# SyncE's issue order changed, and the raw feed-forward weights loaded from GpSimd's queue

## The chip, the core and the metric

The kernel runs on one core of a Trainium2 chip. The core has five engines with a queue each: TensorE (PE in the profile) multiplies matrices, VectorE (DVE), ScalarE (ACT) and GpSimd (POOL) work on rows of 128 partitions, and SyncE (SP) computes nothing and issues DMAs. An engine works its queue off in order; where an instruction waits for a semaphore, everything behind it on that engine waits too. The metric is the device time of one execution in microseconds (us), lower is better.

## The reference

x is [4, 512, 512]. It is normalised and attends, with 32 heads of 16 columns and an axial rotation of q and k, over a context [4, 512, 256]; then comes a feed-forward block whose two weight matrices are cut to three values.

```
q = rope((layernorm(x) @ Wq)); k, v = split(ctx @ Wkv); k = rope(k)
w = softmax(q k^T / 4);  x = x + (w v) @ Wout + bout
xn = layer_norm(layernorm(x));  x_hat = absmax_quant(xn)           # 8 bits
w_hat = sign(round(w / (mean|w| + 1e-6))) * mean|w|                # ternary
h = gelu(x_hat @ w_fc_hat^T);  x = x + absmax_quant(layer_norm(h)) @ w_proj_hat^T
```

All in float32 from outside; the kernel splits float32 operands into bf16 or float32r parts to multiply them exactly enough.

## The kernel before

There are three stages.

Projection (0 to about 150 us): 16 tiles of 128 rows. q and k are rotated, turned, split in three bf16 parts and stored to DRAM (`store_parts`, L270, twelve DMAs for every second tile) from buffers that lie in `ternary_words`, the memory that later holds the turned ternary weights.

Attention (about 140 to 500 us): 32 groups of 4 heads, a batch being 8 groups. For each pair of groups the parts come back as stacks (`load_stacks`, L658): a lower half in 7 DMAs, an upper half in 8, of which the first 3 are q and the last 5 are k. They go round three slots. On TensorE step s does group s - 2. For a group it computes

- scores (`scores`, L748) only to find each row's maximum, one group or more ahead; VectorE reduces them (`row_maxima`, L871);
- scores turned (`scores_turned`, L779), with the row maximum subtracted by two extra rows of the stack; ScalarE takes exponentials;
- the product with the values (`weigh_v`, L795), four chunks in a group, of which the first two are done in the second half of the group's own step and the last two in the first half of the next step.

The maxima take a long way round. GpSimd negates and splits them (`split_maxima`, L902 to L908), SyncE turns them by a DMA transpose (`turn_max`, L668) and stores them into the stack (`load_max`, L672); `scores_turned` of the group waits for that. GpSimd also copies the values of each group into place (`stage_v`, L930), for which `weigh_v` waits.

Beside this a 32nd of the feed-forward weights is made ternary in each step: the raw weights are loaded (`load_weight`, L679 even numbers, w_fc; L682 odd ones, w_proj; two slots), GpSimd cuts them (`ternarise`, L917, L919, L922, two slots of output), SyncE turns them into `ternary_words` by a DMA transpose (`turn_weight`, L688). The second operation of `ternarise(n)` waits until `turn_weight(n - 2)` has landed, and `load_weight(n)` waits for `ternarise(n - 2)`. Since `ternary_words` held the parts, SyncE waits for all stores of parts before the first `turn_weight`.

Finally the rows stage (about 485 us to the end), output product, feed-forward, residuals, in which TensorE is busy nearly throughout.

All orders are written out by hand, one queue for each engine at the end of the kernel. Of SyncE's queue the part from s == TILES + 4 of the first loop and the second loop matter, of GpSimd's the part from `set_pads(pool, 1)`. In a step SyncE issues turn_max, half a pair of stacks, load_max, the raw weight, the sums' transfers (`pack_sums`) and turn_weight. GpSimd does stage_v, split_maxima, ternarise and, in every second step from step 10, a division (L935).

## Time and profile before

| | us |
|---|---|
| median of 3 runs (760.91 to 762.63) | 761.99 |
| the profiled execution's own time | 762.23 |
| its span, first to last instruction | 760.4 |
| TensorE busy in the span | 734.2 |
| VectorE, ScalarE, GpSimd busy | 656.8, 457.1, 432.6 |

The profiled execution spends 1.8 us outside its span. PE is TensorE's matmuls, PEld its weight loads, which overlap them. In the views "SPq" is SyncE issuing a DMA, whose time is that of the issue and not of the transfer. A releaser, written "<-", is what ended an engine's wait. The clock column is TensorE's granted share of full speed: 1.00 is 2.4 GHz, 0.50 is 1.2 GHz.

### The profile page before, as it was taken

How to read it: one execution, taken by the hardware profiler on the slowest of the kernel's cores; microseconds unless marked ns; L12 is line 12 of the kernel's file. 1: busy time of each engine (PE TensorE's matmuls, PEld its weight loads, DVE VectorE, ACT ScalarE, POOL GpSimd, SP SyncE). 2: the span in 40 equal slices, each digit the busy share in tenths (PEclk: the TensorE clock that was granted, in tenths of full speed). 3: DMA queues.
4: the chain of work that ended last, by engine and by line, in shares of the span. 5: the costliest groups of instructions: out<-in, count | busy, mean ns of one | idle time of the engine just before them, and what ended most of it. 6: DMA issues, size and time to landing. Idle time of an engine off the chain costs nothing.

```text
span 760.4 us, 11891 instructions
## 1 busy us (share of the span) xinstructions
PE 734.2 (97%) x3886; PEld 313.9 (41%) x3886; DVE 656.8 (86%) x927; ACT 457.1 (60%) x830; POOL 432.6 (57%) x502
## 2 busy tenths in 40 slices
PE   5999999979999999999999999999999999999998
PEld 3787777412222222222222122445555555555443
DVE  6787998878999999989989787379999889998895
ACT  4786766756777777777777688764224432333330
POOL 5787776754555556654555486466474745663310
PEclk9999999989999999999999999999999999999999
DMA  8798998666577778889888785426657665545546
GB/s 278 191 239 231 256 246 195 150 146 181 137 163 169 166 162 167 162 157 182 151 168 172 171 160 117 94 57 137 119 118 125 119 145 117 105 97 105 117 97 139
DMA packets 185715, 118.05 MB, mean 155 GB/s; under 512 B 120068, under 2 KB 150836, under 8 KB 185652
## 3 DMA queue, kind: packets, MB, share of 16 engines
q1 hardware_dynamic: 185654, 117.29, 69.1%
q8 instruction: 31, 0.51, 0.3%
q14 instruction: 30, 0.25, 0.1%
HBM read 64.50 MB, written 25.43 MB: 118 GB/s over the span
## 4 chain that ended last, share of the span: by engine, by line
PE 77%; SPq 7%; DMA 6%; DVE 3%; issue 2%; ACT 2%; POOL 2%; POOLq 0%; DVEq 0%; ACTq 0%
PE banks L1116 15%; PE banks L1101 15%; PE banks L779 12%; PE banks L795 11%; PE banks L310 9%; PE banks L748 6%; PE banks L1082 6%; SPq L658 4%; DMA stack_words<-k_parts 3%; DVE maxima L871 2%; SPq L270 1%; PE banks L341 1%; DMA late_words<-k_parts 1%; SPq L668 1%; PE banks L765 1%
## 5 line engine op out<-in xcount | busy, mean ns | idle before, releaser
L891 ACT ACTIVATE probs_words<-banks 128x512 f32<-128x512 f32 x512 | 266.0, 603 | 85.9 <-PE banks L779 85.7
L871 DVE TENSOR_REDUCE maxima<-banks 128x2 f32<-128x1024 f32 x240 | 278.4, 1214 | 32.6 <-PE banks L748 31.5
L795 PE MATMUL banks<-probs_words,late_words 128*32 128x512 f32 x1024 | 137.8, 611 | 0.4 <-ACT probs_words L891 0.2
L1101 PE MATMUL banks<-ternary_words,late_words 128*128 128x512 f16 x512 | 113.1, 379 | 0.0
L1116 PE MATMUL banks<-ternary_words,stack_words 128*128 128x512 f16 x512 | 112.9, 379 | 0.0
L779 PE MATMUL banks<-stack_words 114*128 114x512 bf16 x352 | 105.1, 390 | 4.1 <-DMA stack_words<-max_rows 3.9
L1300 ACT ACTIVATE probs_words<-probs_words,h_moments 128x2048 f32<-128x2048 f32 (+1 forms) x17 | 32.2, 1902 | 121.3 <-DVE h_moments L1179 121.3
L1101 PEld LDWEIGHTS banks<-ternary_words,late_words 128*128 128x128 f16 x512 | 49.9, 98 | 60.5 <-issue 0.8
L1116 PEld LDWEIGHTS banks<-ternary_words,stack_words 128*128 128x128 f16 x512 | 49.2, 98 | 60.7 <-issue 2.9
L779 PEld LDWEIGHTS banks<-stack_words 114*128 114x128 bf16 x352 | 26.8, 97 | 91.2 <-ACT probs_words L891 71.4
L1294 ACT ACTIVATE probs_words<-banks,row_scale 128x512 f32<-128x512 f32 x64 | 43.0, 685 | 30.7 <-PE banks L1101 30.7
L748 PE MATMUL banks<-stack_words 48*128 48x512 bf16 x320 | 55.8, 384 | 3.9 <-DMA stack_words<-k_parts 2.1
L902 POOL TENSOR_SCALAR neg_max<-maxima 128x16 f32<-128x16 f32 x32 | 8.3, 260 | 85.1 <-DVE maxima L871 85.1
L1307 POOL TENSOR_TENSOR v_words<-v_words 128x512 f32<-128x512 f32 x16 | 27.0, 1687 | 50.0 <-DMA v_words<-in_x_dram 50.0
L917 POOL TENSOR_SCALAR late_words<-late_words,limits 128x512 f16<-128x512 f32 x32 | 50.2, 1568 | 7.3 <-DMA late_words<-in_L_ffn_w_fc_dram 7.3
L1322 POOL TENSOR_SCALAR v_words<-v_words 128x512 f32<-128x512 f32 x14 | 36.9, 2637 | 26.0 <-DVE late_words L1161 26.0
L544 POOL TENSOR_TENSOR ternary_words<-attn_words,ternary_words 128x512 bf16<-128x512 f32 x32 | 37.3, 1167 | 23.3 <-ACT ternary_words L497 22.6
L919 POOL TENSOR_SCALAR late_words<-late_words,limits 128x512 f16<-128x512 f32 x32 | 50.3, 1572 | 0.0
L779 PE MATMUL banks<-late_words 114*128 114x512 bf16 x160 | 47.0, 384 | 0.0
L540 POOL TENSOR_TENSOR attn_words<-attn_words 128x512 f32<-128x512 f32 x32 | 41.4, 1293 | 2.1 <-DVE attn_words L422 1.9
L748 PEld LDWEIGHTS banks<-stack_words 48*128 48x128 bf16 x320 | 12.7, 93 | 69.6 <-DVE maxima L871 53.4
L1174 DVE BATCH_NORM_STATS2 h_stats<-probs_words 128x6 f32<-128x512 f32 x64 | 39.4, 678 | 0.0
(162 smaller groups left out, 1129.9 us busy)
## 6 DMA issues: line engine op xcount, KB each, us to landing
o_rows<-late_words SPq DMA_DIRECT2D x32, 256.0 KB, 2.9
k_parts<-ternary_words SPq DMA_DIRECT2D x48, 128.0 KB, 3.4
q_parts<-ternary_words SPq DMA_DIRECT2D x48, 128.0 KB, 2.6
stack_words<-q_parts SPq DMA_DIRECT2D x22, 192.0 KB, 3.1
attn_words<-in_x_dram SPq DMA_DIRECT2D x16, 256.0 KB, 5.0
probs_words<-in_L_ffn_w_fc_dram SPq DMA_DIRECT2D x16, 256.0 KB, 3.5
probs_words<-in_L_ffn_w_proj_dram SPq DMA_DIRECT2D x16, 256.0 KB, 5.3
late_words<-in_L_ffn_w_fc_dram SPq DMA_DIRECT2D x16, 256.0 KB, 3.7
```

Of the source, the lines that this page charges most:

```text
L310: mm = self.nc.tensor.matmul(out, lhs[a][:, slot, k * P:(k + 1) * P], rhs[b][:, k, :], start=(a + b + k == 0), stop=(a == 1 and k == count ...
L748: mm = self.nc.tensor.matmul(self.score_slot[j % 2][:, half], self.stack(0, g)[rows, head, c * P:(c + 1) * P], self.stack(1, g)[rows, head ...
L779: self.nc.tensor.matmul(self.st_bank[(g * 16 + k) % self.ST_BANKS], self.stack(1, g)[0:STACK, head, c * P:(c + 1) * P], self.stack(0, g)[0 ...
L795: mm = self.nc.tensor.matmul(self.pv_bank[32 * j:32 * j + 32], self.v_ones[:, g % 2, c, j, :], self.probs[:, c, j, :], start=(c == 0), sto ...
L871: dve.tensor_reduce(self.maxima[:, g % 2].rearrange("p (x i) -> p x i", x=2)[:, :, j], self.score_slot[j % 2], AX.X, ALU.max).then_inc(sel ...
L891: act.activation(self.probs[:, c, head, :], self.st_bank[(g * 16 + k) % self.ST_BANKS], ACT.Exp, scale=1 / math.sqrt(HEAD)).then_inc(self. ...
L917: pool.tensor_scalar(self.below[:], self.raw[:, w], limits[:, 1, w:w + 1], None, ALU.is_lt).then_inc(self.cut, 1)
L919: pool.tensor_scalar(self.ternary[:, w], self.raw[:, w], limits[:, 0, w:w + 1], None, ALU.is_gt).then_inc(self.cut, 1)
L1082: mm = self.nc.tensor.matmul(self.y_bank[n % 2], self.mixT[n % 2][a][:, k], self.wout_parts[b][:, k, :], start=(a + b + k == 0), stop=(a = ...
L1101: mm = self.nc.tensor.matmul(self.fc_bank[o], self.uT[:, n % U_SLOTS, part * KX + k], self.fcT[:, k, o], start=(k + part == 0), stop=(k == ...
L1116: mm = self.nc.tensor.matmul(self.proj_bank[r], self.hT[:, r, part, k], self.projT[:, k // 2, k % 2], start=(k + part == 0), stop=(part == ...
L1294: act.activation(self.h[:, n % H_SLOTS, o * DIM:(o + 1) * DIM], self.fc_bank[o], ACT.Gelu, scale=self.row_scale[:, n % U_SLOTS]).then_inc( ...
```

## The change

Four things in SyncE's queue, and one that leaves it for GpSimd's.

- Maxima of group 2: turn_max(2) and load_max(2) stood behind the last tile's twelve stores and behind the wait for all stores. Now turn_max(2) stands before these stores and load_max(2) in their middle.
- Upper halves of stacks: all 8 DMAs stood in the even step. Now the 3 of q are issued in the odd step before, behind load_max, and the 5 of k stay.
- Raw weights: the two before the loop and one in each step are gone from SyncE. GpSimd issues them: numbers 0 and 1 behind set_pads(1), and number n + 2 behind ternarise(n).
- The four pieces of Wout are loaded two in each of two steps instead of one in each of four.

TensorE's, VectorE's and ScalarE's queues are the same.

```diff
@@ -259,12 +259,12 @@
-    def store_parts(self, sp, n):
+    def store_parts(self, sp, n, which=slice(0, 2 * PARTS)):
...
-        for s, part in ((0, 0), (0, 1), (1, 0), (0, 2), (1, 1), (1, 2)):
+        for s, part in ((0, 0), (0, 1), (1, 0), (0, 2), (1, 1), (1, 2))[which]:
...
-    def load_stacks(self, sp, pair, half):
+    def load_stacks(self, sp, pair, half, both=(0, 1)):
...
-        for t, where, runs in ((0, mem.q_parts, self.Q_RUNS[half]), (1, mem.k_parts, self.K_RUNS[half])):
+        for t in both:
+            where, runs = ((mem.q_parts, self.Q_RUNS[half]), (mem.k_parts, self.K_RUNS[half]))[t]
...
-    def load_weight(self, sp, w_fc, w_proj, n):
+    def load_weight(self, queue, w_fc, w_proj, n):
         half = n % 4 // 2
-        need(sp, self.ternary_ready, n - 1)
+        need(queue, self.ternary_ready, n - 1)
...
@@ -1373,14 +1374,16 @@
                 if s == TILES + 4:
                     sp.wait_ge(prj.projected[1], TILES)
-                    att.load_weight(sp, w_fc, w_proj, 0)
-                    att.load_weight(sp, w_fc, w_proj, 1)
                     att.turn_max(sp, 1)
                     att.begin_late_stacks(sp)
                     att.load_stacks(sp, STACK_PAIRS - 1, 0)
                     att.load_max(sp, 1)
                     att.load_stacks(sp, STACK_PAIRS - 1, 1)
-                if within(s - 5, TILES) and (s - 5) % 2 == 1:
+                    att.turn_max(sp, 2)
+                    prj.store_parts(sp, TILES - 1, slice(0, PARTS))
+                    att.load_max(sp, 2)
+                    prj.store_parts(sp, TILES - 1, slice(PARTS, 2 * PARTS))
+                if within(s - 5, TILES - 1) and (s - 5) % 2 == 1:
                     prj.store_parts(sp, s - 5)
...
@@ -1394,24 +1397,24 @@
-                if s == 3:
-                    att.turn_max(sp, 2)
-                    att.load_max(sp, 2)
                 if 5 <= s < GROUPS + 2:
                     att.turn_max(sp, s - 2)
-                if 2 * STACK_PAIRS <= s + 1 < GROUPS:
-                    att.load_stacks(sp, (s + 1) // 2, (s + 1) % 2)
+                if 2 * STACK_PAIRS <= s + 1 < GROUPS and s % 2 == 1:
+                    att.load_stacks(sp, (s + 1) // 2, 0)
+                if 2 * STACK_PAIRS <= s < GROUPS and s % 2 == 0:
+                    att.load_stacks(sp, s // 2, 1, (1,))
                 if 5 <= s < GROUPS + 2:
                     att.load_max(sp, s - 2)
-                if 2 <= s < GROUPS:
-                    att.load_weight(sp, w_fc, w_proj, s)
+                if 2 * STACK_PAIRS <= s + 1 < GROUPS and s % 2 == 1:
+                    att.load_stacks(sp, (s + 1) // 2, 1, (0,))
                 att.pack_sums(sp, s)
...
-                if GROUPS - 6 <= s < GROUPS - 2:
-                    rows.load_weight(sp, wout, s - GROUPS + 6)
+                if s in (GROUPS - 6, GROUPS - 4):
+                    for k in range(2):
+                        rows.load_weight(sp, wout, s - GROUPS + 6 + k)
...
@@ -1713,12 +1716,17 @@
             att.set_pads(pool, 1)
+            pool.wait_ge(prj.projected[1], TILES)
+            for n in range(2):
+                att.load_weight(pool, w_fc, w_proj, n)
             att.stage_v(pool, 1)
             prj.weigh_ffn(pool)
             pool.tensor_scalar(rows.gamma_128[:], mem.gammas[:], 1 / Q_B, None, ALU.mult).then_inc(prj.gamma_step, 1)
             att.ternarise(pool, 0)
+            att.load_weight(pool, w_fc, w_proj, 2)
             att.split_maxima(pool, 2)
             att.ternarise(pool, 1)
+            att.load_weight(pool, w_fc, w_proj, 3)
             for s in range(2, GROUPS + 1):
...
                 if s < GROUPS:
                     att.ternarise(pool, s)
+                if s + 2 < GROUPS:
+                    att.load_weight(pool, w_fc, w_proj, s + 2)
```

SyncE's queue at the end of the projection, before: the last four of the twelve stores (L270), then the raw weight 2, the first turned weights and the maxima of group 2.

```order
L270 DMA q_parts<-ternary_words 64x4x256 [waits q_second_done]
L270 DMA q_parts<-ternary_words 64x4x256
L270 DMA q_parts<-ternary_words 64x4x256 [waits q_third_done]
L270 DMA q_parts<-ternary_words 64x4x256
L679 DMA late_words<-in_L_ffn_w_fc_dram 128x512 [waits ternary_ready,parts_stored_1,parts_stored_0]
L688 DMA_TRANSPOSE ternary_words<-late_words 128x4x128 [waits ternary_ready]
L668 DMA_TRANSPOSE max_rows<-max_parts 128x128 [waits max_loaded_0,pads_ready,split_ready]
L672 DMA stack_words<-max_rows 2x16x128 [waits max_turned_0]
L682 DMA late_words<-in_L_ffn_w_proj_dram 128x2x256 [waits ternary_ready]
L688 DMA_TRANSPOSE ternary_words<-late_words 128x4x128 [waits ternary_ready]
```

After, from the place where the pair 2's stacks are loaded:

```order
L669 DMA_TRANSPOSE max_rows<-max_parts 128x128 [waits max_loaded_0,pads_ready,split_ready]
L270 DMA k_parts<-ternary_words 64x4x256 [waits k_first_done]
L270 DMA k_parts<-ternary_words 64x4x256
L270 DMA k_parts<-ternary_words 64x4x256 [waits k_second_done]
L270 DMA k_parts<-ternary_words 64x4x256
L270 DMA q_parts<-ternary_words 64x4x256 [waits q_first_done]
L270 DMA q_parts<-ternary_words 64x4x256
L673 DMA stack_words<-max_rows 2x16x128 [waits max_turned_0]
L270 DMA k_parts<-ternary_words 64x4x256 [waits k_third_done]
L270 DMA k_parts<-ternary_words 64x4x256
L270 DMA q_parts<-ternary_words 64x4x256 [waits q_second_done]
L270 DMA q_parts<-ternary_words 64x4x256
```

Two more stores and the first turn_weight (L689, with the wait for all parts) follow these. The transpose of group 2's maxima went from behind the stores to before them, and turn_weight(0) is still behind all twelve.

GpSimd's queue from ternarise(1) on, before: two ternarisings, the values of group 2 (L930), the split of group 3's maxima.

```order
L917 TENSOR_SCALAR late_words<-late_words,limits 128x512 [waits ternary_ready,raw_loaded_1]
L919 TENSOR_SCALAR late_words<-late_words,limits 128x512
L922 TENSOR_TENSOR late_words<-late_words 128x512 [waits cut]
L917 TENSOR_SCALAR late_words<-late_words,limits 128x512 [waits ternary_ready,raw_loaded_0]
L919 TENSOR_SCALAR late_words<-late_words,limits 128x512 [waits wT_turned_0]
L922 TENSOR_TENSOR late_words<-late_words 128x512 [waits cut]
L930 COPY late_words<-v_words 128x16x16 [waits pv_done]
L902 TENSOR_SCALAR neg_max<-maxima 128x16 [waits scores_read]
L905 TENSOR_SCALAR max_parts<-neg_max 128x16 [waits neg_ready,max_turned_1]
L908 TENSOR_TENSOR max_parts<-neg_max,max_parts 128x16 [waits high_ready]
```

After:

```order
L918 TENSOR_SCALAR late_words<-late_words,limits 128x512 [waits ternary_ready,raw_loaded_1]
L920 TENSOR_SCALAR late_words<-late_words,limits 128x512
L923 TENSOR_TENSOR late_words<-late_words 128x512 [waits cut]
L683 DMA late_words<-in_L_ffn_w_proj_dram 128x2x256 [waits ternary_ready]
L918 TENSOR_SCALAR late_words<-late_words,limits 128x512 [waits ternary_ready,raw_loaded_0]
L920 TENSOR_SCALAR late_words<-late_words,limits 128x512 [waits wT_turned_0]
L923 TENSOR_TENSOR late_words<-late_words 128x512 [waits cut]
L680 DMA late_words<-in_L_ffn_w_fc_dram 128x512 [waits ternary_ready]
L931 COPY late_words<-v_words 128x16x16 [waits pv_done]
L903 TENSOR_SCALAR neg_max<-maxima 128x16 [waits scores_read]
L906 TENSOR_SCALAR max_parts<-neg_max 128x16 [waits neg_ready,max_turned_1]
L909 TENSOR_TENSOR max_parts<-neg_max,max_parts 128x16 [waits high_ready]
```

A DMA with a wait for the ternary result just made stands behind each ternarising, and the copy of values and the split of maxima stand behind it.

SyncE's queue in two later steps, before: turn_weight, then an even step with the upper half of pair 3 (q, then k) between turn_max (L668) and load_max (L672).

```order
L688 DMA_TRANSPOSE ternary_words<-late_words 128x4x128 [waits ternary_ready]
L668 DMA_TRANSPOSE max_rows<-max_parts 128x128 [waits max_loaded_2,pads_ready,split_ready]
L658 DMA stack_words<-q_parts 48x2x1024 [waits st_ready,parts_stored_1,parts_stored_0]
L658 DMA stack_words<-q_parts 16x2x1024
L658 DMA stack_words<-q_parts 32x2x1024
L658 DMA stack_words<-k_parts 16x2x1024 x3
L658 DMA stack_words<-k_parts 32x2x1024
L658 DMA stack_words<-k_parts 16x2x1024
L672 DMA late_words<-max_rows 2x16x128 [waits max_turned_0]
L679 DMA late_words<-in_L_ffn_w_fc_dram 128x512 [waits ternary_ready]
L693 DMA o_rows<-late_words 128x512 [waits o_saved]
```

After, from load_max of the odd step:

```order
L673 DMA stack_words<-max_rows 2x16x128 [waits max_turned_1]
L659 DMA stack_words<-q_parts 48x2x1024 [waits st_ready,parts_stored_1,parts_stored_0]
L659 DMA stack_words<-q_parts 16x2x1024
L659 DMA stack_words<-q_parts 32x2x1024
L694 DMA o_rows<-late_words 128x512 [waits o_saved]
L689 DMA_TRANSPOSE ternary_words<-late_words 128x4x128 [waits ternary_ready]
L669 DMA_TRANSPOSE max_rows<-max_parts 128x128 [waits max_loaded_2,pads_ready,split_ready]
L659 DMA stack_words<-k_parts 16x2x1024 [waits st_ready,parts_stored_1,parts_stored_0]
L659 DMA stack_words<-k_parts 16x2x1024 x2
L659 DMA stack_words<-k_parts 32x2x1024
L659 DMA stack_words<-k_parts 16x2x1024
L673 DMA late_words<-max_rows 2x16x128 [waits max_turned_0]
```

The q part of the upper half went into the odd step, before its o_rows store, and only k stands between turn_max and load_max of the even step.

## Rows read from the trace of the kernel before

**Rows 1.** The page's first line: the span of the profiled execution.
```profile
span 760.4 us, 11891 instructions
```

**Rows 2.** TensorE's waits, 140 to 500 us: total, times, longest.
```profile
PE banks L779 <- DMA stack_words<-max_rows: 3.9, 1, 3.9
PE banks L748 <- DMA late_words<-k_parts: 2.2, 2, 1.7
PE banks L748 <- DMA stack_words<-k_parts: 2.1, 4, 1.0
```

**Rows 3.** Windows: stretch, length, busy time by engine, TensorE clock, DMA share, GB/s.
```profile
168.00:172.00 4.00, 4.00 (x16) 0.47 (x14) 2.36 (x2) 2.17 (x4) 3.76 (x7) 0.50 0.79 208
200.00:280.00 80.00, 80.00 (x485) 18.75 (x483) 74.69 (x73) 62.53 (x122) 45.16 (x57) 1.00 0.72 159
280.00:470.00 190.00, 184.97 (x1111) 43.36 (x1113) 172.04 (x166) 145.78 (x284) 109.14 (x134) 0.99 0.82 163
400.00:440.00 40.00, 38.11 (x224) 8.83 (x224) 34.63 (x34) 29.43 (x58) 18.62 (x27) 0.96 0.79 173
```

**Rows 4.** Timeline of TensorE before the long wait: start, duration, instruction.
```profile
162.50 1.07 PE L795 MATMUL banks<-probs_words,late_words 128*32 128x512 f32 x8
```

**Rows 5.** Chain of waits, 159 to 194 us: start, us, what.
```profile
159.25 2.40 DMA q_parts<-ternary_words
...
165.78 1.97 DMA stack_words<-max_rows
...
174.57 0.99 PE banks L795 x8
...
182.73 0.99 PE banks L795 x8
...
193.28 1.00 PE banks L795 x8
```

**Rows 6.** SyncE's timeline: start, us, issue (late stores, then group 3's maxima).
```profile
151.88 2.67 SPq L270 DMA_DIRECT2D k_parts<-ternary_words  x4
...
161.70 0.37 SPq L679 DMA_DIRECT2D late_words<-in_L_ffn_w_fc_dram  x1
...
171.22 1.16 SPq L668 DMA_TRANSPOSE max_rows<-max_parts  x1
...
175.86 0.67 SPq L672 DMA_DIRECT2D stack_words<-max_rows  x1
...
288.42 2.30 SPq L658 DMA_DIRECT2D late_words<-k_parts  x5
```

**Rows 7.** GpSimd's timeline: start, us, instruction, idle time before it and its releaser.
```profile
145.07 0.31 POOL L926 MEMSET late_words<- 128x256 f32 x1
...
151.96 0.27 POOL L902 TENSOR_SCALAR neg_max<-maxima 128x16 f32<-128x16 f32 x1 [0.88 <-DVE maxima L871]
...
164.56 1.57 POOL L917 TENSOR_SCALAR late_words<-late_words,limits 128x512 f16<-128x512 f32 x1 [7.27 <-DMA late_words<-in_L_ffn_w_fc_dram]
...
167.76 1.15 POOL L922 TENSOR_TENSOR late_words<-late_words 128x512 f16<-128x512 f16 x1
...
186.22 0.40 POOL L930 COPY late_words<-v_words 128x256 f32<-128x256 f32 x1 [1.77 <-PE banks L795]
189.69 0.26 POOL L902 TENSOR_SCALAR neg_max<-maxima 128x16 f32<-128x16 f32 x1 [3.08 <-DVE maxima L871]
```

**Rows 8.** DMA view, 140 to 500 us: transposes of ternary weights, median us to landing.
```profile
ternary_words<-late_words SPq DMA_TRANSPOSE x32, 3.7
```

**Rows 9.** The page's groups: GpSimd's slowest operation, busy, mean ns, idle before it.
```profile
L1322 POOL TENSOR_SCALAR v_words<-v_words 128x512 f32<-128x512 f32 x14 | 36.9, 2637 | 26.0 <-DVE late_words L1161 26.0
```

**Rows 10.** Chain of waits, the last load of pair 8's upper half.
```profile
290.29 4.66 DMA late_words<-k_parts
```

**Rows 11.** Windows around it, columns as in rows 3.
```profile
281.00:285.00 4.00, 4.00 (x26) 0.98 (x22) 3.93 (x5) 2.86 (x6) 0.66 (x2) 1.00 0.59 179
288.00:291.00 3.00, 3.00 (x21) 0.72 (x23) 3.00 (x4) 2.35 (x6) 2.92 (x3) 1.00 1.08 143
```

More of the change, by code:

```diff
@@ L673, in load_max @@
                      self.max_rows[0:2 * GH * CHUNKS, g % 2]).then_inc(self.max_loaded[g % STACK_SLOTS], DMA)
-    def load_weight(self, sp, w_fc, w_proj, n):
+    def load_weight(self, queue, w_fc, w_proj, n):
         half = n % 4 // 2
-        need(sp, self.ternary_ready, n - 1)
+        need(queue, self.ternary_ready, n - 1)
         if n % 2 == 0:
-            sp.dma_start(self.raw[:, 0], w_fc.rearrange("(i h p) d -> h i p d", h=2, p=P)[half, n // 4]
+            queue.dma_start(self.raw[:, 0], w_fc.rearrange("(i h p) d -> h i p d", h=2, p=P)[half, n // 4]
                          ).then_inc(self.raw_loaded[0], DMA)
         else:
-            sp.dma_start(self.raw[:, 1].rearrange("p (r c) -> p r c", r=2),
+            queue.dma_start(self.raw[:, 1].rearrange("p (r c) -> p r c", r=2),
                          w_proj.rearrange("(h r p) (i c) -> h i p r c", h=2, p=P, c=2 * P)[half, n // 4]
```

## The prediction

> **What bounds the kernel now.** I read the page's first line first, then the windows. The span is 760.4 us [rows 1]; in 200 to 280 us TensorE is busy 80.00 of 80 us [rows 3], although VectorE is near too (74.69). In the rows stage TensorE runs nearly throughout. So the time is TensorE's work plus what TensorE loses, and the change alters no TensorE instruction: I look only for the losses that SyncE's and GpSimd's queues cause.
>
> TensorE's waits [rows 2] name two. One is a single wait of 3.9 us for max_rows, the maxima of group 2. The others are loads of k parts, 4.3 us in six waits, the longest 1.7.
>
> The first loss is larger than its wait. The products with the values follow each other at a fixed beat, 2.88 and 2.40 us in turn, and the same place of the next step comes 10.55 us later (182.73 to 193.28) [rows 5]. The product at 162.50 [rows 4] should be followed two places later by one at 167.78; it is the one at 174.57 [rows 5]. That is 6.8 us. The wait is 3.9 of it, and 2.9 are the clock, which stands at 0.50 after the wait [rows 3], i.e. 1.2 instead of 2.4 GHz.
>
> The second loss: from 280 to 470 us TensorE is idle 190.00 - 184.97 = 5.03 us, and the clock of 0.96 over 400 to 440 costs 0.04 x 40 = 1.6 more [rows 3]. Together 6.6 us. Its pattern is one pair of groups: the last of the upper half's 8 loads is issued at 290.29 and lands 4.66 later [rows 10], and TensorE goes on then.
>
> **Part 1: the wait for group 2's maxima.** It goes if load_max(2) lands before 163.9 (167.8 less 3.9). Before, turn_max(2) stood behind the stores. The new chain begins on GpSimd.
>
> What GpSimd pays for issuing a DMA, D, is in no row. From below: SyncE's issue of the same load takes 0.37 us [rows 6]. From above: GpSimd's slowest operation takes 2.64 us [rows 9]. I take 1.2, the level of its ordinary operations on 128x512 (1.15 and 1.57) [rows 7]. A load lands 2.86 us after SyncE begins its issue (161.70, with GpSimd going on at 164.56) [rows 6, 7], so 2.5 us after its end.
>
> - set_pads(1) ends at 145.38 [rows 7]. Loads 0 and 1 take it to 147.8; load 0 ends at 146.6 and lands at 149.1. The copy of values (0.40) and four operations on limits (estimate 0.9 in all, none longer than the 0.27 of the smallest in [rows 7]) also end at 149.1.
> - ternarise(0) takes 4.35 (164.56 to 168.91) [rows 7]: 153.5. Load 2, with a wait for its own result: 154.7. The split is three such small operations with their waits, an estimate of 1.0: 155.7. VectorE has been done since 151.96 [rows 7], so GpSimd is late, not VectorE.
> - SyncE reaches turn_max(2) at 151.9, where the stores began [rows 6], and idles until 155.7. Then 1.16 for the transpose and six stores of 0.67 (2.67 for four) [rows 6]: load_max(2) at 160.9, landed 1.97 later [rows 5] at 162.8. That is 1.1 us early: the wait goes, and so does the slow clock behind it. Gain 6.8 us.
>
> **Part 2: what is late next.** The twelve stores now end later, and turn_weight(0) is behind them all. The last store is issued at 155.7 + 1.16 + 0.67 + 11 x 0.67 = 164.9 and lands 2.40 later [rows 5]: 167.3. A transpose of weights lands in 3.7 us in the median [rows 8], a store on this stretch's quiet queue in 2.40 [rows 5]; I take 3.0: 170.4. Only then may the second operation of ternarise(2) run, with the third 2.75 us: 173.15. Load 4 (1.25): 174.4. The values of group 2 are copied at 174.8, and group 3's maxima are split at 175.8.
>
> TensorE, no longer stopped at 163.9, wants group 2's values at 177.45 - 6.8 = 170.65 (two places, 2.88 us, behind the 174.57 of [rows 5]) and group 3's maxima 3.8 us after that, 174.45. It waits 4.1 us for the values, as long as it waited before, so I give it the same half clock: 3.8 us of work then ends at 174.8 + 3.8 + 2.9 = 181.5. The maxima: load_max(3) comes 4.64 us behind turn_max(3) (171.22 to 175.86) [rows 6], so 180.5, landed at 182.4. TensorE begins group 3's turned scores at 182.4 instead of 174.45. Loss 8.0 us. Against Part 1's 6.8, the start of attention is 1.2 us worse. Each further us of D enters three times (loads 0, 2, 4).
>
> **Part 3: the upper halves.** The 3 loads of q leave the path from maximum to stack. They carry 384 KB (96 rows of 2 x 2 KB). At the 143 GB/s of 288 to 291 us [rows 11] this is 2.7 us. They move to where DMA engines stood at 0.59 [rows 11] and there is room for (1 - 0.59) x 4 = 1.6 us; 1.1 us comes back as a later start. The k loads land at least 1.6 us earlier; by the issue time alone 1.45. The longest wait is 1.7 [rows 2], so almost everything goes, the clock drop behind it too. I keep 0.4 of 6.6: gain 6.2.
>
> **Part 4: the rest.** In a steady step GpSimd idles 1.77 us before the copy and 3.08 before the split [rows 7], 4.85 together; D hides there, and in steps with a division (of one 128x512 operation, 1.2 to 1.6 by [rows 7]) some 3.5 are left. TensorE's wait would come back with D over that. A load issued by SyncE cost 0.4 us of a queue that had slack. Moving Wout's loads only regroups them: 0.
>
> **Sum.** The profiled execution took 762.23, 1.8 outside its span. 762.2 - 6.8 + 8.0 - 6.2 = 757.2. It lay 0.2 above the median of the runs, which I count as nothing: 757.2.
>
> What a page says of D stands apart. The Trainium skill, "DMA: Bandwidth & Descriptors", section "Anatomy of one DMA — SWDGE (gpsimd) path", puts the dispatch at some 50 ns and calls the generation of descriptors small at first; by it D would be near my lower bound and the sum 2.4 lower. No run shows this yet.
>
> **Rivals.**
>
> 1. The q loads help only in part, because their bytes come back as backlog: six waits shortened by 0.4 each, a gain of 2.4 instead of 6.2, 761.0. For it speaks the share of 1.08 at 288 to 291 us, against it the room at 0.59 [rows 11].
>
> 2. Slower: the raw weights no longer queue behind the k loads but run beside them. w_fc's load is issued when ternarise ends, just while the k loads are landing. Its 256 KB at 143 GB/s are 1.8 us; if all its packets go ahead, the k loads lose 1.8 and win only the 1.4 us of three issues (2.30 for five) [rows 6]. Then each of 8 pairs waits 0.4 longer, +3.2, and the sum is 762.2 + 1.2 + 3.2 = 766.6. It decides from the point where what goes ahead exceeds that 1.4. Against it: loads land in 2.86 when nothing else is on, so most of their packets should fit between.
> That DMAs of all issuers share the same 16 engines and interleave, and that issuing elsewhere saves only the issue time, is what the Trainium skill says ("DMA: Bandwidth & Descriptors", section "Issuing engines are not separate DMA queues"); the trace has one issuing queue and can't show it.
>
> 3. GpSimd is held far longer, D = 3.5 or with a start-up cost at the first use. Part 2 grows by 3 x 2.3 = 6.9: 764.1. It is slower from about D = 3.4. Nothing in the trace speaks for so much; nothing excludes it.
>
> 4. The start also gains: D at 0.4 takes 2.4 from the chain, 754.8.
>
> **Chances.** Forecast 0.50, by itself 754.5 to 760.4; rival 1 0.15; rival 2 0.15; rival 3 0.12; rival 4 0.08. The 0.2% that a measurement can tell is 1.5 us, so faster means below 760.5 and slower above 763.5. Faster: 0.48 of the forecast, 0.06 of rival 1, 0.08 of rival 4, 0.62 together. Slower: 0.14 of rival 2 and 0.08 of rival 3, 0.22. The same: 0.16. The range takes the small-D case in at the bottom (754) and stops at 765.5 before the whole of rival 2.
>
> **What would show it.** TensorE's wait at 163.9 gone; one of about 4 us near 171 for GpSimd's copy of values, a half clock after it, and a short one at about 182 for max_rows. GpSimd idle before the second operation of ternarise(2). From 280 to 470 us fewer than 1 us of waits for k parts and no second drop of the clock. A GpSimd step without longer splits. I am wrong if TensorE waits for maxima or values after 200 us, if the k waits stay with w_fc's packets beside them, or if an issue on GpSimd takes over 2 us.

## The result, and the profile after

The changed kernel took 765.91 us (median of 10 runs, 763.9 to 767.57) beside 761.84 us of the kernel before on the same chip (10 runs). The ratio is 1.0044 with a 95% interval of 1.0023 to 1.0064: slower, where 757.2 us and faster were forecast. The profiled execution took 766.85 us.

The page's head, then TensorE's waits from 140 to 500 us, which answer to [rows 1, 2]:

```profile
span 765.0 us, 11904 instructions
```

```profile
PE banks L796 <- issue: 5.2, 1, 5.2
PE banks L780 <- DMA stack_words<-max_rows: 3.5, 2, 3.1
PE banks L749 <- DMA late_words<-k_parts: 1.4, 1, 1.4
PE banks L749 <- DMA stack_words<-k_parts: 0.9, 2, 0.5
```

The waits for k parts fell from 4.3 to 2.3 us. The one long wait of the start, 3.9 us, became two, of 5.2 and 3.1, beside a short one of 0.39. TensorE's timeline shows where (start, duration, instruction, idle time before it):

```profile
166.53 0.60 PE L780 MATMUL banks<-stack_words 114*128 114x512 bf16 x2 [0.39 <-DMA stack_words<-max_rows]
...
178.66 1.93 PE L796 MATMUL banks<-probs_words,late_words 128*32 128x512 f32 x8 [5.18 <-issue]
...
187.63 1.03 PE L780 MATMUL banks<-stack_words 114*128 114x512 bf16 x2 [3.11 <-DMA stack_words<-max_rows]
```

"Issue" stands there because the profile found no releaser; the instruction is weigh_v, and GpSimd had copied its values at 178.56 (178.14 and 0.42, below). The windows that answer to [rows 3]:

```profile
168.00:172.00 4.00, 4.00 (x27) 0.93 (x26) 4.00 (x4) 2.73 (x7) 0.00 (x0) 1.00 0.52 113
200.00:280.00 80.00, 80.00 (x490) 18.67 (x483) 74.60 (x72) 62.48 (x122) 49.65 (x62) 1.00 0.79 159
280.00:470.00 190.00, 187.74 (x1139) 44.15 (x1137) 175.68 (x169) 149.62 (x290) 123.50 (x156) 1.00 0.83 170
400.00:440.00 40.00, 38.61 (x235) 9.22 (x237) 36.00 (x36) 29.94 (x59) 26.45 (x33) 1.00 0.83 174
```

The clock drop at 400 to 440 us is gone (0.96 before, 1.00 now), and TensorE is busy 187.74 of 190 us against 184.97 before. So the long stretch gained, and the loss lies in the first 60 us of attention. The chain of waits goes through it without a gap; these are its pieces (start, us, what):

```profile
146.39 5.62 DMA late_words<-in_L_ffn_w_fc_dram
152.17 1.58 POOL late_words L918
...
158.55 1.14 SPq L669
159.74 0.68 SPq L270
...
167.80 2.43 DMA q_parts<-ternary_words
170.29 4.05 DMA ternary_words<-late_words
174.42 1.58 POOL late_words L920
...
178.14 0.42 POOL late_words L931
179.55 1.12 SPq L669
...
184.14 3.44 DMA stack_words<-max_rows
187.58 0.05 issue
187.63 1.03 PE banks L780 x2
```

Read downwards: the first raw load, ternarise(0), turn_max(2), the twelve stores with load_max(2) between them, turn_weight(0), the rest of ternarise(2), the values, turn_max(3), load_max(3), TensorE. GpSimd's timeline has the new issues, which [rows 7] could not show:

```profile
146.39 0.79 POOL L680 DMA_DIRECT2D late_words<-in_L_ffn_w_fc_dram  x1
147.19 0.75 POOL L683 DMA_DIRECT2D late_words<-in_L_ffn_w_proj_dram  x1
...
152.17 1.58 POOL L918 TENSOR_SCALAR late_words<-late_words,limits 128x512 f16<-128x512 f32 x1 [2.83 <-DMA late_words<-in_L_ffn_w_fc_dram]
...
156.84 0.64 POOL L680 DMA_DIRECT2D late_words<-in_L_ffn_w_fc_dram  x1 [0.30 <-POOL late_words L923]
...
174.42 1.57 POOL L920 TENSOR_SCALAR late_words<-late_words,limits 128x512 f16<-128x512 f32 x1 [8.85 <-DMA ternary_words<-late_words]
```

In this execution TensorE's clock also stood at half for some 3 us during group 0, where it stood at full speed in the kernel before (third column from the end):

```profile
146.00:149.00 3.00, 3.00 (x12) 0.31 (x10) 2.90 (x3) 1.09 (x2) 2.81 (x8) 0.50 1.05 196
```

Group 0 took 14.0 us by it instead of 12.8. The chain above doesn't pass through TensorE between 146 and 187 us, so these 1.2 us only shortened the wait that follows. Of the kernels below, "maxima before weights" and the one with a small DMA behind turn_weight have this drop too, and "stacks whole again", whose queues are the same up to there, lacks it; so it is put down to the execution and not to the change.

To compare executions I cut each span at three matmuls: the first turned score of group 0, of group 4 and of group 31 (16 of L779 a group). Behind group 31 every kernel of this study takes 274.9 to 275.1 us, so two stretches tell everything. Medians and ratios are of the timed runs, each against the kernel before on its own chip; the stretches are of one execution. Two cautions belong to them. In the executions of eight kernels whose start is ordered as before but for small DMAs (before itself, the split alone, raw from 2 on GpSimd, w_proj a step later, and the four with a small DMA) the first stretch took 49.8 to 52.8 us, so 1 to 2 us in that column say nothing. And the kernel before was 2.6 to 3.4 us slower on the chips of the experiments (medians of 764.5 to 765.2) than on the chip of its own trace (761.8), so a stretch of an experiment isn't strictly comparable with the 293.9 of before; where the two disagree, the ratio of the medians decides. The changed kernel was timed on the first chip alone. Two single executions of the experiments, of 1195 and 2493 us, lie far outside and are left out of the ratios.

| kernel | 0 to 4 | 4 to 31 | median | ratio, 95% |
|---|---|---|---|---|
| before | 51.1 | 293.9 | 761.8 | |
| changed | 59.3 | 289.3 | 765.9 | 1.0044 (1.0023 to 1.0064) |
| all raw weights on SyncE | 54.3 | 293.9 | 769.2 | 1.0054 (1.0030 to 1.0077) |
| first two on SyncE | 54.4 | 290.7 | 762.9 | 0.9970 (0.9953 to 0.9987) |
| stacks whole again | 57.2 | 288.7 | 766.0 | 1.0020 (0.9996 to 1.0043) |
| maxima before weights | 56.8 | 290.9 | 766.4 | 1.0017 (0.9994 to 1.0040) |
| before, split alone | 49.8 | 297.7 | 765.8 | 1.0021 (0.9998 to 1.0043) |
| before, raw on GpSimd | 51.9 | 290.7 | 759.6 | 0.9931 (0.9905 to 0.9957) |
| before, raw from 2 on GpSimd | 50.0 | 290.2 | 759.8 | 0.9929 (0.9905 to 0.9953) |
| start rearranged | 46.0 | 292.1 | 754.9 | 0.9860 (0.9832 to 0.9889) |

Before and after in one sum: 762.2 + 8.2 (start) - 4.6 (27 groups) + 1.1 (group 0 begins at 141.5 instead of 140.4) = 766.9, against 766.85.

### The profile page after: what moved, and what is told of

The parts are those of the page before. It is cut to its first block, busy times and chain, and to the rows that moved or that the text cites. A ratio compares the mean times of both kernels' runs of the same rounds, so it can differ in the third digit from the quotient of the medians.

```text
span 765.0 us, 11904 instructions
## 1 busy us (share of the span) xinstructions
PE 736.1 (96%) x3886; PEld 313.7 (41%) x3886; DVE 657.8 (86%) x927; ACT 457.3 (60%) x830; POOL 455.7 (60%) x534
## 4 chain that ended last, share of the span: by engine, by line
PE 80%; SPq 7%; DMA 6%; POOL 2%; ACT 2%; DVE 2%; issue 1%; DVEq 0%; POOLq 0%; ACTq 0%
PE banks L1117 14%; PE banks L1102 14%; PE banks L780 13%; PE banks L796 13%; PE banks L310 8%; PE banks L749 7%; PE banks L1083 6%; SPq L659 3%; DMA stack_words<-k_parts 2%; SPq L270 1%; PE banks L341 1%; PE banks L766 1%; PE banks L293 1%; SPq L669 1%; DMA q_parts<-ternary_words 1%
## 5 line engine op out<-in xcount | busy, mean ns | idle before, releaser
L749 PEld LDWEIGHTS banks<-stack_words 48*128 48x128 bf16 x320 | 12.8, 93 | 67.5 <-DVE maxima L872 54.2
```

The costliest lines, as they stand in the source:

```text
L749: mm = self.nc.tensor.matmul(self.score_slot[j % 2][:, half], self.stack(0, g)[rows, head, c * P:(c + 1) * P], self.stack(1, g)[rows, head ...
```

## The experiments

**One part of the change at a time.** The kernel before had a median of 764.5 us on this chip (29 runs).

All raw weights back on SyncE:

```diff
-            for n in range(2):
-                att.load_weight(pool, w_fc, w_proj, n)
...
+                    att.load_weight(sp, w_fc, w_proj, 0)
+                    att.load_weight(sp, w_fc, w_proj, 1)
                     att.turn_max(sp, 1)
...
+                if 2 <= s < GROUPS:
+                    att.load_weight(sp, w_fc, w_proj, s)
                 att.pack_sums(sp, s)
```

> The changed kernel with the raw weights back on SyncE: loads 0 and 1 ahead of turn_max(1), load n in step n behind load_max; everything else as changed. Theory A (the start is lost because the raw loads of the software queue land late beside SyncE's loads, which holds ternarise(0) until 156.5 and with it split(2)): ternarise(0) ends near 151, turn_max(2) is issued near 154 instead of 158.6, group 3 begins 4 to 5 us earlier than the 187.6 of the changed kernel, and the steady part keeps its gain; the median is 760 to 762, 4 to 6 below the changed kernel. Theory B (SyncE's new order at the start alone is the cause: the twelve stores and turn_weight(0) behind turn_max(2), whoever issues the raw loads): group 3 begins within 1.5 us of 187.6 and the median is 764 to 767. Theory C (the software queue costs in the steady part): the stretch 200 to 485 is over 1 us shorter than in the changed kernel.

769.18 us, above the medians of both A and B. ternarise(0) ended 10.6 us after group 0 began, against 15.0 in the changed kernel, and the start was 5.0 us shorter: that part of theory A held. But the stretch behind it took 293.9 us, as before the change. Theory C has the wrong sign: raw loads on GpSimd gain there.

Raw weights from GpSimd alone, SyncE's order otherwise as before:

```diff
             att.ternarise(pool, 0)
+            att.load_weight(pool, w_fc, w_proj, 2)
...
-                if 2 <= s < GROUPS:
-                    att.load_weight(sp, w_fc, w_proj, s)
```

> The kernel before with SyncE's order untouched and only the raw weights issued by GpSimd. Theory A: split(2) becomes late, about 158.5, but turn_max(2) stands behind the stores at 163.6 and doesn't notice; the start is within 1.5 us of before, the waits for k parts stay or shrink by less than half; median 760 to 764. Theory C (the packets of the raw weights beside k loads make them later): waits for k parts grow by 0.4 us a pair, median 764 to 767.

759.58 us, ratio 0.9931, just under what theory A gave. In its execution the long stretch is 3.2 us shorter; the start is 0.8 us longer, which is within the scatter of that column.

Only raw loads 0 and 1 back on SyncE (they count on semaphores of their own; so they do in the later versions that have them there):

```diff
-            for n in range(2):
-                att.load_weight(pool, w_fc, w_proj, n)
...
+                    att.load_weight(sp, w_fc, w_proj, 0)
+                    att.load_weight(sp, w_fc, w_proj, 1)
                     att.turn_max(sp, 1)
```

> The changed kernel with only raw loads 0 and 1 back on SyncE ahead of turn_max(1); loads 2 to 31 stay with GpSimd. Theory A: ternarise(0) no longer waits for its raw load and ends near 151.5, split(2) near 153.5, turn_max(2) near 154; group 3 begins 3 to 5 us earlier than 187.6; median 761 to 763, between the changed kernel and the one with all on SyncE. Theory B: no change, 764 to 767.

762.88 us, as theory A gave. Against the changed kernel the ratio falls from 1.0044 to 0.9970: two of 32 loads are worth 0.74%, 5.6 us. These two ratios come from different chips, and their intervals leave some 2 us either way; the start itself is 4.9 us shorter. Against all on SyncE (1.0054, same chip) the thirty later loads are worth 0.84%, 6.4 us. TensorE's wait before weigh_v is down to 1.0 us, and the profile puts it down to ScalarE; the wait for group 3's maxima has grown to 6.4:

```profile
173.15 1.07 PE L796 MATMUL banks<-probs_words,late_words 128*32 128x512 f32 x8 [1.02 <-ACT probs_words L892]
...
183.32 1.03 PE L780 MATMUL banks<-stack_words 114*128 114x512 bf16 x2 [6.39 <-DMA stack_words<-max_rows]
```

Only the split of the upper halves, in the kernel before:

```diff
-                if 2 * STACK_PAIRS <= s + 1 < GROUPS:
-                    att.load_stacks(sp, (s + 1) // 2, (s + 1) % 2)
+                if 2 * STACK_PAIRS <= s + 1 < GROUPS and s % 2 == 1:
+                    att.load_stacks(sp, (s + 1) // 2, 0)
+                if 2 * STACK_PAIRS <= s < GROUPS and s % 2 == 0:
+                    att.load_stacks(sp, s // 2, 1, (1,))
                 if 5 <= s < GROUPS + 2:
                     att.load_max(sp, s - 2)
+                if 2 * STACK_PAIRS <= s + 1 < GROUPS and s % 2 == 1:
+                    att.load_stacks(sp, (s + 1) // 2, 1, (0,))
```

> The kernel before with one edit: the upper halves of a pair's stacks are loaded as k ahead of load_max and q behind it. All theories agree that the start stays as before. By the traces of before and after the stretch from group 4 to the end of attention is 4.7 us shorter (its waits for k parts and the clock drop at 426); I expect 756 to 758.5, 0.992 to 0.996 of before. Rival (the gain of the steady part comes from the raw weights leaving SyncE, not from the split): the waits for k parts stay, 761 to 763.

765.81 us: no gain, and the waits for k parts grew from 4.3 to 6.0 us. The expectation, that the steady gain comes from the split, is wrong. SyncE's timeline, GpSimd's and the end of the chain show why, for the same pair as [rows 10]:

```profile
281.49 2.07 SPq L659 DMA_DIRECT2D late_words<-q_parts  x3
283.61 0.43 SPq L683 DMA_DIRECT2D late_words<-in_L_ffn_w_proj_dram  x1
...
285.93 1.25 SPq L689 DMA_TRANSPOSE ternary_words<-late_words  x1
287.29 1.22 SPq L669 DMA_TRANSPOSE max_rows<-max_parts  x1
288.62 2.39 SPq L659 DMA_DIRECT2D late_words<-k_parts  x5
```

```profile
286.14 0.22 POOL L909 TENSOR_TENSOR max_parts<-neg_max,max_parts 128x16 bf16<-128x16 f32 x1
```

```profile
290.58 6.27 DMA late_words<-k_parts
296.86 0.09 issue
```

The last k load took 6.27 us to land instead of 4.66, and the weights' transpose of 285.93 landed after 8.1 us where the one of 283.93 took 5.6. The three q loads no longer stand directly ahead of the k loads, but now ahead of the transposes, which are ahead of the k loads. In this stretch the weights' transpose landed at 294.0, the maxima's at 294.5 and the k loads from about 294.9 to 296.9, in the order of their issue, so much the same bytes were still in front of the last k load.

SyncE itself was a second reason. The split of the maxima ended at 286.36 (286.14 and 0.22), but turn_max went only at 287.29: SyncE was busy from 281.49 on without a pause, because the three q loads take it 2.07 us in the odd step, beside the raw load. Over the 21 steps from 200 to 425 us turn_max was issued 0.8 us behind the split in the mean here, 0.75 us with the split and all raw weights on SyncE, 0.3 us in the changed kernel, and 0.06 us in the kernel before. So the split of the stacks and the raw loads together are more than SyncE's step holds.

**Which waits make the start.** The kernel before: 764.8 us (25 runs). First, GpSimd copies group 2's values and splits group 3's maxima before ternarise(2):

```diff
             att.ternarise(pool, 1)
             att.load_weight(pool, w_fc, w_proj, 3)
+            att.stage_v(pool, 2)
+            att.split_maxima(pool, 3)
             for s in range(2, GROUPS + 1):
-                if s >= 3:
+                if s >= 4:
                     att.stage_v(pool, s - 1)
```

> The changed kernel with two steps of GpSimd exchanged at the start: it copies group 2's values and splits group 3's maxima before ternarise(2) instead of behind it. If the chain of Part 2 holds (the values wait for ternarise(2), which waits for turn_weight(0), which stands behind the twelve stores), the wait of 5.2 us for the values at 178.7 goes and group 3 begins 5 to 8 us before 187.6; its maxima may then be bounded by SyncE, where turn_max(3) stands behind turn_weight(0) and turn_weight(1) at about 173. Median 5 to 8 us below the changed kernel, 758 to 761. If the values waited for something else, or the loss is the late load of the maxima, group 3 begins within 2 us of 187.6.

766.39 us, not the 758 to 761 expected. The wait for the values is gone, as expected, and one wait of 8.3 us took the place of both. SyncE's timeline and TensorE's say where it came from:

```profile
175.99 1.21 SPq L689 DMA_TRANSPOSE ternary_words<-late_words  x1
177.30 1.16 SPq L669 DMA_TRANSPOSE max_rows<-max_parts  x1
```

```profile
185.85 0.61 PE L780 MATMUL banks<-stack_words 114*128 114x512 bf16 x1 [8.32 <-DMA stack_words<-max_rows]
```

By GpSimd's timeline the maxima were split at 165.65, but turn_max(3) waits in SyncE's queue behind turn_weight(2), which waits for ternarise(2). I had named this bound in the expectation and put it at 173, with turn_weight(0) and (1); the third transpose, at 176, is the one. The chain through ternarise(2) has two branches; cutting one left the other.

Second, the stacks in one piece again, all other edits kept:

```diff
-                if 2 * STACK_PAIRS <= s + 1 < GROUPS and s % 2 == 1:
-                    att.load_stacks(sp, (s + 1) // 2, 0)
-                if 2 * STACK_PAIRS <= s < GROUPS and s % 2 == 0:
-                    att.load_stacks(sp, s // 2, 1, (1,))
+                if 2 * STACK_PAIRS <= s + 1 < GROUPS:
+                    att.load_stacks(sp, (s + 1) // 2, (s + 1) % 2)
...
-                if 2 * STACK_PAIRS <= s + 1 < GROUPS and s % 2 == 1:
-                    att.load_stacks(sp, (s + 1) // 2, 1, (0,))
```

> The changed kernel with the upper halves of the stacks loaded in one piece again, ahead of load_max as before; all other edits stay. The earlier run with only the split gave no gain, so the theory now is that the raw weights' leaving SyncE's queue makes the steady gain, and the split costs: loads land in the order of their issue, and the q loads moved forward lengthen the odd steps' backlog, in which the weights' transposes land after 6 to 8 us. By it the stretch from group 4 to group 31 stays at 289 to 291 us or gets up to 3 us shorter, median 762 to 766. The prediction's theory (the split gives the steady gain) has the waits for k parts back at 4.3 us and the median at 768 to 772.

766.01 us. The long stretch took 288.7 us without the split and 289.3 with it; the ratios, 1.0020 and 1.0044, overlap in their intervals. So the split is worth nothing that these runs can tell, in either kernel.

Third, a start that serves both branches:

```diff
+                    prj.store_parts(sp, TILES - 1, slice(0, PARTS))
                     att.turn_max(sp, 2)
-                    prj.store_parts(sp, TILES - 1, slice(0, PARTS))
-                    att.load_max(sp, 2)
                     prj.store_parts(sp, TILES - 1, slice(PARTS, 2 * PARTS))
+                    att.load_max(sp, 2)
...
-                if within(s - 2, GROUPS):
-                    att.turn_weight(sp, s - 2)
+                for n in ([], [s - 2], [2, 3])[0 if s == 4 else 2 if s == 5 else 1]:
+                    if within(n, GROUPS):
+                        att.turn_weight(sp, n)
```

with GpSimd's exchange above, raw loads 0 and 1 on SyncE and the stacks whole.

> A version meant to beat both. Raw weights 0 and 1 on SyncE ahead of turn_max(1), 2 to 31 on GpSimd; six stores ahead of turn_max(2) and six behind it, load_max(2) after them; GpSimd copies values 2 and splits maxima 3 before ternarise(2); turn_weight(2) goes behind turn_max(3); stacks whole. If the losses at the start are the waits named (values behind ternarise(2), maxima 2 behind the stores), group 4 begins near 186, 5 us before the 191.5 of the kernel before, with no or one half-clock stretch, and the rest takes 290 to 291 us: 752 to 756. If a further wait takes their place (load_max(3) landing behind stack loads, which are issued ahead of it), group 4 begins at 189 to 192 and the median is 757 to 760.

754.91 us, ratio 0.9860, as expected: faster than both kernels. The start is 5.1 us shorter than before, which is half of the 1.4%; the other half is what the later raw weights on GpSimd gave by themselves (0.7%, the next run). Group 3's maxima are now late by half a microsecond, and the clock stays at full speed from 140 to 200 us:

```profile
175.63 0.61 PE L780 MATMUL banks<-stack_words 114*128 114x512 bf16 x2 [0.50 <-DMA stack_words<-max_rows]
```

```profile
140.00:200.00 60.00, 57.14 (x336) 14.23 (x336) 53.83 (x53) 44.84 (x88) 43.98 (x56) 1.00 0.65 170
```

Fourth, the kernel before with raw weights 2 to 31 from GpSimd (the raw-on-GpSimd edit, without its first two loads):

> The kernel before, SyncE's order untouched, with only raw weights 2 to 31 issued by GpSimd. Compared with all 32 on GpSimd (759.6 beside 764.5) the start should get back its 0.8 us: group 4 begins 51.1 us after group 0, not 51.9, and the rest takes 290 to 291 us; median 757.5 to 760, 0.990 to 0.994 of before. If the steady gain of that run was chance (a clock drop that before had and it had not), the median is 762 to 765.

759.82 us, as with all 32. The gain repeats on a second chip (0.9931 and 0.9929, both intervals below 0.996), so it isn't chance; the first two loads don't matter where turn_max(2) stands behind the stores anyway.

**What the thirty later loads cost SyncE.** The kernel before: 764.5 us (22 runs). A small DMA in each place that a raw load left:

```diff
+                if 2 <= s < GROUPS:
+                    sp.dma_start(mem.small_rows[s], w_fc[0:P, 0:16]).then_inc(prj.w_loaded["pos"], DMA)
```

> The version with raw weights 2 to 31 on GpSimd and SyncE's order of before, plus a small DMA on SyncE in each place from which a raw load left: 128 rows of 64 bytes from DRAM to DRAM, nothing waits for it. It gives SyncE back an issue of some 0.4 to 0.7 us and the queue 128 small descriptors, but not the 256 KB. Group 4 to group 31 took 293.9 us before and 290.2 without the raw loads on SyncE. If the gain came from SyncE's shorter step, the stretch is 293 to 295 and the median 762 to 765; if it came from the 256 KB that no longer stand in SyncE's hardware queue ahead of the k loads, it stays at 289.5 to 291 and the median at 759 to 761.

763.51 us, 0.9989 (0.9964 to 1.0014): most of the gain is gone without any of the 256 KB, as the theory of SyncE's step had it. The stretch, 292.3 us, lies between the two theories. But SyncE wasn't late: in 19 of the 21 steps from 200 to 425 us turn_max followed the split within 0.1 us, as in the kernel before. So the cost doesn't come through the start of turn_max.

All raw weights on SyncE, w_proj's a step later:

```diff
-                if 2 <= s < GROUPS:
-                    att.load_weight(sp, w_fc, w_proj, s)
+                for n in ([s] if s < 5 else [s - 1, s] if s % 2 == 0 else []):
+                    if 2 <= n < GROUPS:
+                        att.load_weight(sp, w_fc, w_proj, n)
```

> The kernel before, all raw weights on SyncE; only the loads of w_proj (odd n, from 5 on) are issued one step later, behind the k loads instead of ahead of them, together with the even step's w_fc. SyncE issues as much in all. If 256 KB standing ahead of the k loads in the queue is what made TensorE wait, the waits for k parts fall below 2 us, the stretch from group 4 to group 31 is 289 to 291.5 and the median 758.5 to 761.5 beside 764.5 of before. If it is SyncE's issue time or the sum of bytes, the waits stay near 4.3 us and the median within 1.5 of before; a new wait is possible in ternarise of odd n, whose raw load then lands only about when GpSimd wants it.

759.67 us, 0.9933 (0.9909 to 0.9958): the whole gain, with every raw load still on SyncE. So the gain doesn't need the loads to leave SyncE; it is enough that w_proj's stands behind the k loads instead of ahead of them. Its waits for k parts, 4.0 us in the profiled execution, did not fall below 2 as expected, and its long stretch took 292.1 us; the median tells more here than the one trace.

The rearranged start with raw loads 0 and 1 on GpSimd too:

> The rearranged start (754.9 beside 764.8) with one difference: raw weights 0 and 1 also come from GpSimd. By the landings of the changed kernel ternarise(0) then ends near 156.5 instead of 151.8 and split(2) near 158.5 instead of 153.9. SyncE's first six stores end at 156.5, so turn_max(2) goes at 158.5, load_max(2) at about 163.8 instead of 161.8, turn_weight(0) at 166, and everything behind it 2 to 4 us later than with the two loads on SyncE; split(3) near 170 instead of 163.7. Group 4 begins 2 to 5 us later, median 756.5 to 760. If the landing of those two loads matters only for the start as the change had it, the median is within 1 us of 754.9.

755.43 us, 0.9876 (0.9841 to 0.9912): within 1 us of 754.9, the second of the two cases. The start took 47.6 us instead of 46.0, and the stretch behind it 289.5 instead of 292.1. Load 0 landed as late as in the changed kernel (6.1 us), so the late first loads cost much only where everything queues behind them.

Last, the small DMA in odd steps only, in even steps only, and in every step but behind turn_weight (before: 765.2 us, 29 runs):

```diff
-                if 2 <= s < GROUPS:
+                if 2 <= s < GROUPS and s % 2 == 1:
```

> As the run with a small load in place of each raw load, but only in odd steps, where w_proj's load stood: ahead of the weights' transpose, the next step's transpose of maxima and its k loads, which all land in order. If what is issued there in odd steps makes TensorE wait, nearly the whole 4.6 us come back: median 762.5 to 764 beside 764.5 of before. If the place doesn't matter but the number of DMAs does, half comes back: 761.5 to 762.5.

> The same with the small load only in even steps, behind the k loads, where the queue drains before anything urgent: by the theory of place no cost, median 759.5 to 761, as without small loads (759.8); by the theory of number 761.5 to 762.5.

> A small load in every step again, but behind the weights' transpose at the end of the step. By the theory that the transposes' landing is what is held up, it costs less than in front of them, but it still stands ahead of the next step's transpose of maxima and k loads: 760.5 to 762.5. By the theory of number 763 to 764.5, as ahead of it.

762.01 us (0.9962, interval 0.9937 to 0.9988), 760.26 us (0.9941, 0.9911 to 0.9970) and 767.58 us (1.0025, 0.9991 to 1.0060). Number alone fits badly: against 0.9929 without them, thirty cost 0.6% in one place and 1.0% in another. It isn't refuted, because the intervals of these two overlap. The even steps cost 0.1%, which is nothing that these runs can tell. The odd ones took back about 0.3% of 0.7, less than I expected, with an interval that reaches the even ones'. My guess for the last run had the wrong sign. SyncE's timeline in it, then GpSimd's, at the step of [rows 10]:

```profile
287.63 1.25 SPq L689 DMA_TRANSPOSE ternary_words<-late_words  x1
288.93 0.59 SPq L1414 DMA_DIRECT2D small_rows<-in_L_ffn_w_fc_dram  x1
289.63 1.17 SPq L669 DMA_TRANSPOSE max_rows<-max_parts  x1
```

```profile
289.15 0.22 POOL L909 TENSOR_TENSOR max_parts<-neg_max,max_parts 128x16 bf16<-128x16 f32 x1
```

Between turn_weight's end at 288.88 and the split's end at 289.37 SyncE has 0.5 us to spare. A 0.59 us issue with the gaps around it doesn't fit, turn_max and the k loads go 0.3 us later, and TensorE's waits for k parts in this execution were 9.1 us. It is so in 20 of the 21 steps from 200 to 425 us, 0.4 us in the mean. That is a part of the cost and not shown to be all of it: 0.4 us in each of the 13 pairs that the loop loads would be some 5 us, an estimate, and the ratio rose by 1.0%, 7.3 us.

Ahead of turn_weight SyncE has more slack. In the kernel before it idles 0.9 us between these two:

```profile
280.53 0.78 SPq L682 DMA_DIRECT2D late_words<-in_L_ffn_w_proj_dram  x1
282.21 0.34 SPq L693 DMA_DIRECT2D o_rows<-late_words  x1
```

So an issue there should cost nothing, and turn_max indeed went no later; yet it took back most of the gain. Whether that comes through the landing of the small packets or through the steps after group 24 is open; one execution of each kernel scatters by as much as the question is worth.

## Why the prediction was wrong

It forecast 4.8 us less than before, and the kernel took 4.1 us more. By its own steps:

- **GpSimd's price, D = 1.2.** Right within 0.3: 0.64 us for w_fc and 0.79 for w_proj, each behind 0.30 of waiting for its own result. Rival 3 (3.5) and rival 4 (0.4) are both out. (By its own numbers rival 3 is slower from D = 3.3, not 3.4.) The Trainium skill's 50 ns for the dispatch ("DMA: Bandwidth & Descriptors", section "Anatomy of one DMA — SWDGE (gpsimd) path") is not what GpSimd is held for here; the rows above have 640 to 790 ns.
- **Part 1, the landing of load 0.** The first step that failed. I took 3.7 us from issue to landing, from a load that was alone in the queue [rows 6, 7]. It took 5.62, beside fifteen of SyncE's stack loads, and 5.8 to 6.1 in four other executions with the same issue. ternarise(0) ended at 156.54 instead of 153.5: 1.9 us by this landing, and 1.0 because this execution was that much later already when GpSimd came to the issue (146.4 for 145.4). Every later member of the chain moved with it: turn_max(2) 158.55 for 155.7, the last landing of the stores 170.2 for 167.3. The run with two loads moved back puts 5.6 us, give or take 2, on issue and landing of the two together. The wait for group 2's maxima still went, all but 0.39 us, as predicted.
- **Part 2, what is late next.** The chain is the one forecast, member for member: GpSimd waiting for turn_weight(0), TensorE for the values, a half clock, then a wait for the maxima. Its sizes were off. load_max(3), behind seven stack loads, landed after 3.44 us, not 1.97; in four other kernels it took 3.3 to 4.6 at this place, so this term was too small. turn_weight(0) landed after 4.05 us, not 3.0; in five other kernels it took 2.5 at this place, so that miss belongs to this execution. TensorE began group 3 46.1 us after group 0 instead of 42, and the clock was at half again from 186.8 to 193.6, which made group 3 take 13.2 us instead of 10.6: 2.6 us that I had not counted. In all 8.2 us of loss where 1.2 was forecast. The window of that second drop in the changed kernel, clock 0.50 in the third column from the end:

```profile
187.00:193.00 6.00, 5.37 (x19) 0.77 (x20) 2.36 (x2) 2.17 (x4) 4.19 (x4) 0.50 1.10 188
```

- **Part 3, the upper halves.** Wrong in its cause. The stretch gained 4.6 us of the 6.2, but the split alone gained nothing (1.0021), and taking it out cost nothing. That the sum came so near here is luck: the gain is that of Part 4. I had counted 2.7 us of q data as out of the way behind load_max; in that pair's landings they only changed what they delayed. And I left out what their issue costs SyncE in the odd step, which made turn_max 0.8 us late in the mean where the raw loads stayed. Rival 1, the bytes that come back as backlog, was this step's right form, even too mild.
- **Part 4, the raw loads' leaving SyncE.** Priced at 0, "a queue that had slack", and it is the whole steady gain: 0.7% of before in two series. Rival 2, w_fc's packets making the k loads late, is refuted by the same runs (its 8 pairs were also too few; the loop loads 13). The Trainium skill ("DMA: Bandwidth & Descriptors", section "Issuing engines are not separate DMA queues") holds that issuing elsewhere saves only the issue. A small issue of 0.6 us put back took 4.6 of 5.4 us again, which agrees; that the same gain came with every raw load still issued by SyncE, only w_proj's behind the k loads, doesn't. That points at what stands ahead of the k loads in the odd step; by which way a small DMA there costs so much no run settled. The regrouping of Wout's loads, also put at 0, was in no run changed by itself.

For the profiled execution the misses add up: 757.2 + 1.9 (landing of load 0) + 1.0 (turn_weight(0)) + 1.5 (load_max(3)) + 2.6 (second half clock) + 1.1 (group 0 later) + 1.6 (the long stretch) = 766.9; what else was off by a few tenths cancels.

The measured 765.9 us lies just outside the range, which stopped at 765.5 before the whole of rival 2. The chance of slower was 0.22, given to two mechanisms that did not occur; a slower case made of my own chain with landings of a loaded queue was missing.

## What to carry to other kernels

When an instruction waits in an ordered queue, price the landings from rows in which that queue is as full as it will be at that moment: along one chain, 1.9 and 1.5 us too little on two landings, and a second stretch of half clock behind the wait that they lengthened, took away the gain that was forecast. Moving a load forward in such a queue doesn't take its bytes away from what follows; look at what it now stands ahead of, and whether the issuing engine has time for it in that step. And before cutting a wait, follow all branches from the late event: taking the values out from behind ternarise(2) gained nothing until turn_max(3) was out too, and then both together, with the stores reordered, made the start 5.1 us shorter than before the change.

## What the runs showed of the hardware

GpSimd's loads go through a queue of their own kind. The DMA view of the changed kernel (queue, packets, MB, share; then KB each and median us to landing):

```profile
q1 hardware_dynamic: 55370, 47.40, 65.5%
q0 software_dynamic: 2560, 8.39, 9.2%
```

```profile
late_words<-in_L_ffn_w_fc_dram POOLq DMA_DIRECT2D x16, 256.0 KB, 4.0
late_words<-in_L_ffn_w_proj_dram POOLq DMA_DIRECT2D x16, 256.0 KB, 5.1
```

A 256 KB load was issued in 0.64 or 0.79 us of GpSimd's time and landed 4.0 to 5.1 us later in the median, but 5.6 and 7.1 us later for the first two, beside fifteen of SyncE's loads, and 2.9 to 3.6 us later for the next three, before SyncE's next loads.

I had not expected that an issue of 0.6 us (128 rows of 64 bytes) in SyncE's queue, which nothing waits for, costs 0.6% in every step and 1.0% behind the weights' transpose, but only 0.1% in the even steps; each of these figures can be off by some 0.4%.
